# A two-layer convolution block: transforming 32 normalized channels in place of 85 projected ones

## The chip, the core and the metric

The kernel runs on one core of a Trainium2 chip. TensorE (PE) multiplies, VectorE (DVE), ScalarE (ACT) and GpSimd (POOL) do the elementwise work, SyncE (SP) issues most transfers. The metric is device time in microseconds; three runs of the kernel before gave 830.47 (828.88 to 832.42).

## What is computed

Two layers of the same block, each with a residual, on x of shape 4 x 32 x 128 x 128, with HID = 85 and 8 x 8 patches. `_gn` with 32 groups on 32 channels normalizes each channel of each image over its pixels.

```python
def _forward(x, W_in, W_dw, fft_weight, W_out):
    xm = jnp.einsum('bchw,oc->bohw', x, W_in)
    x_spatial, x_freq, x_gate = jnp.split(xm, 3, axis=1)
    out_spatial = depthwise 3x3 convolution of x_spatial with W_dw
    xf = jnp.fft.rfft2(patches of x_freq)
    xf = xf * fft_weight
    xi = jnp.fft.irfft2(xf, s=(P, P))
    out_freq = xi back in image order
    x_fused = jax.nn.gelu(x_gate, approximate=False) * (out_spatial + out_freq)
    return jnp.einsum('bchw,oc->bohw', x_fused, W_out)
...
x = x + layer0(_gn(x)); x = x + layer1(_gn(x))
```

The projection acts on channels and the patch transform on pixels, so the two can be done in either order.

## The kernel before

The image is cut into four bands of 32 columns (Q = 4), and the 128 partitions are 4 bands x 32 channels. A strip is 8 columns wide in each band and 128 rows high; a tile is 16 x 8 = 128 pixels (two patches) of each band. There are 8 tiles in a strip, 32 strips (ALL) and 256 tiles in both layers. All operands of the f16 matmuls are split into a high and a low part, and products of high with high, high with low and low with high are summed.

For each strip DVE normalizes (`normalize`, L812), ACT and DVE split it in three horizontal shifts (L544 and L836, `parts`), and 28 transfers of SP (L273 in pairs, L279 in thirds) put the parts of one band into `stack`, with channels and shifts stacked on 128 partitions. A stack serves as stationary operand, so each tap matmul has the 85 columns of its weights as moving operand. Strip s+1 is loaded from the first step of strip s on, when strip s-1 has left its buffer.

One loop over steps i runs on every engine, each with its own order, with semaphores between them. On PE a step is: taps of band 0 for tile i (`conv(i, 0)`, 7 matmuls, L395); the turned product `ps_ft` of tile i-2 (L442); in each fourth step (i % 4 = 2) the output product `ps_o` of four tiles (L453); half of the gate's projection (L401, `ps_g`); band 1; the projection of the frequency part of tile i+3 (L401, `ps_u`); the rest of the gate; band 2; the patch transform of tile i+2 (L482 to L485, `ps_z`, three matmuls of 340 columns over `uh` and `ul`); band 3; and the inverse transform of tile i into the same bank as the taps (L490 to L493). In short, tile by tile:

- ACT copies `ps_u` scaled to f16 (`uh`, L585) and DVE takes the rest (`ul`, L925).
- DVE multiplies `ps_z` by the weights of the spectrum (`y`, L931), ACT and POOL split that into `yh` (L594) and `yl` (L654) for the inverse.
- ACT applies Gelu (L589), DVE multiplies taps plus inverse by it (`f`, L895), ACT copies the turned product (L579), DVE adds four tiles' output to x (L905) and, in layer 0, takes statistics of them (L774).
- POOL sends and gathers statistics (L616, L622) and edges (L634, L643) in some 15 steps up to step 141.

The last instruction of each step of PE releases the next: `f` of tile i-1 must be done before step i+1 uses the bank, `yl` of tile i+2 before the end of step i+2. At the start the first strip comes in two pieces (`load_piece`) over three queues, and PE runs 32 matmuls of no use (L384) before the loop.

Of the kernel before, what the change touches and what calls it, by code (L numbers as in the profile page):

```python
# [14 lines left out]
LAYERS = 2  # L15
# [25 lines left out]
LEAD = 3  # L41
DRAIN = 4
WARM = 32

OUT = 4
KH = P * (P // 2 + 1)
# [22 lines left out]
FIRST_LOADS = [(PAIRS_HI[0::2], PAIRS_LO[0::2], THIRDS[0::3]), (PAIRS_HI[1::2], PAIRS_LO[1::2], THIRDS[1::3]),  # L69
               ([], [], THIRDS[2::3])]  # L70
# [7 lines left out]
SUMMING = {1: range(8), 2: (17, 21, 24, 25, 29, 32, 33, 37), 3: (49, 53, 56, 57, 61, 64, 65, 69)}  # L78


def build(nc, x_in, edges_in, w_raw, w_fft, w_out, basis, inverse, squares, fold, sums, y_out):
    ctx = ExitStack()
    with ctx:
# [18 lines left out]
        inv = sb("inv", [128, 2, 128], F16)  # L102
        squares_sb = sb("squares_sb", [128, 2, 128])
# [3 lines left out]
        apart = sb("apart", [128, Q, 2 * STRIPS * 6])  # L107
        fold_sb = sb("fold_sb", [KH, 128])

        raw = [sb(f"raw{i}", [128, 12 * HID]) for i in range(LAYERS)]  # L110
        win = [r[:, 0:3 * HID] for r in raw]
        wdw = [r[:, 3 * HID:] for r in raw]
        fft = [sb(f"fft{i}", [KH, HID]) for i in range(LAYERS)]
# [20 lines left out]
        gathered = sb("gathered", [128, Q, 2 * STRIPS * 6])  # L134
        inside = sb("inside", [128, 2])
# [8 lines left out]
        uh = sb("uh", [128, 2, GC], F16)  # L144
        ul = sb("ul", [128, 2, GC], F16)
# [5 lines left out]
        ft = sb("ft", [HID, 2 * OUT, Q, 128])  # L151
# [4 lines left out]
        ps_u = [bank("ps_u0"), bank("ps_u1")]  # L156
        ps_g, ps_z, ps_ft, ps_o = (bank(n) for n in ("ps_g", "ps_z", "ps_ft", "ps_o"))
# [3 lines left out]
        folded = [ps_u[0][:, 0:HID], ps_o[:, 128:128 + HID]]  # L161
# [50 lines left out]
        s_u = sem("s_u")  # L212
        s_uh = sem("s_uh")
        s_ul = sem("s_ul")
# [35 lines left out]
        def staged(i, parts_of_a_strip):  # L250

            if i < 0:
                at = 2 * (i + LEAD)
                return 1, [p for p in parts_of_a_strip.values() if at <= p < at + 2 or i == -1 and p > at]
            strip, at = i // TPS + 2, i % TPS
            return strip, [parts_of_a_strip[at]] if at in parts_of_a_strip and strip < ALL else []
# [40 lines left out]

        def load_piece(eng, piece, by):

            (hi, lo, thirds), loaded = FIRST_LOADS[by], s_first[piece][by]  # L300
# [731 lines left out]
```

## Time and profile before

| | |
|---|---|
| three runs, median | 830.47 us |
| the profiled execution | 829.37 us |
| its span, first to last instruction | 827.6 us |
| PE busy | 799.3 us (97%) |
| DVE busy | 612.7 us (74%) |
| ACT busy | 571.5 us (69%) |
| POOL busy | 274.4 us (33%) |
| mean granted clock of TensorE | 0.993 |

Busy time is that of the engine's own instructions; time spent in waiting or in issuing transfers from SP and ACT does not count. Matmuls are pipelined, each shown longer than the distance to the next one, so the cost of one is read from the distance between starts. A timeline merges equal neighbours, with their count behind the x.

### The profile page before, as it was taken

How to read it: one execution, taken by the hardware profiler on the slowest of the kernel's cores; microseconds unless marked ns; L12 is line 12 of the kernel's file. 1: busy time of each engine (PE TensorE's matmuls, PEld its weight loads, DVE VectorE, ACT ScalarE, POOL GpSimd, SP SyncE). 2: the span in 40 equal slices, each digit the busy share in tenths (PEclk: the TensorE clock that was granted, in tenths of full speed). 3: DMA queues.
4: the chain of work that ended last, by engine and by line, in shares of the span. 5: the costliest groups of instructions: out<-in, count | busy, mean ns of one | idle time of the engine just before them, and what ended most of it. 6: DMA issues, size and time to landing. Idle time of an engine off the chain costs nothing.

```text
span 827.6 us, 31423 instructions
## 1 busy us (share of the span) xinstructions
PE 799.3 (97%) x12332; PEld 654.8 (79%) x12332; DVE 612.7 (74%) x1153; ACT 571.5 (69%) x1149; POOL 274.4 (33%) x345
## 2 busy tenths in 40 slices
PE   1799999999999999999999999999999999999997
PEld 0588888888888888888888888888888888888885
DVE  7887888888888777687777776667667766767553
ACT  2566676767767777777777777677776777777664
POOL 2724232542336322433234223332232333223221
PEclk9799999999999999999999999999999999999999
DMA  8766557545555445655454665655665655566621
GB/s 295 181 210 145 135 125 211 133 113 128 134 125 140 110 111 118 144 132 130 109 118 114 158 141 142 157 131 134 149 141 146 156 133 134 138 142 156 150 63 51
DMA packets 66522, 115.51 MB, mean 140 GB/s; under 512 B 16242, under 2 KB 18954, under 8 KB 65994
## 3 DMA queue, kind: packets, MB, share of 16 engines
q1 hardware_dynamic: 63606, 110.50, 54.1%
q0 software_dynamic: 2144, 2.59, 1.3%
q8 instruction: 99, 1.62, 0.9%
q10 hardware_dynamic: 628, 0.43, 0.2%
q14 instruction: 45, 0.37, 0.1%
HBM read 10.98 MB, written 8.56 MB: 24 GB/s over the span
## 4 chain that ended last, share of the span: by engine, by line
PE 94%; DVE 3%; issue 1%; DMA 1%; ACT 1%; SPq 0%; POOL 0%; DVEq 0%; ACTq 0%
PE ps_s L395 35%; PE ps_ft L442 15%; PE ps_o L453 8%; PE ps_g L401 6%; PE ps_u L401 5%; PE ps_z L482 5%; PE ps_s L490 5%; PE ps_s L493 4%; PE ps_s L491 4%; PE ps_z L485 4%; PE ps_z L483 4%; DMA x<-in_x 1%; DVE parts L836 1%; DVE st L755 0%; DVE amax L685 0%
## 5 line engine op out<-in xcount | busy, mean ns | idle before, releaser
L395 PE MATMUL ps_s<-cw,stack 128*128 128x85 f16 (+1 forms) x7168 | 457.5, 203 | 0.4 <-DVE f L895 0.4
L395 PEld LDWEIGHTS ps_s<-cw,stack 128*128 128x128 f16 (+1 forms) x7168 | 379.4, 98 | 49.1 <-DVE f L895 0.8
L654 POOL TENSOR_TENSOR yl<-y,yh 128x340 f16<-128x340 f32 x256 | 230.0, 899 | 525.4 <-ACT yh L594 525.4
L594 ACT ACTIVATE yh<-y 128x340 f16<-128x340 f32 x256 | 124.7, 487 | 195.6 <-DVE y L931 124.2
L925 DVE SCALAR_TENSOR_TENSOR ul<-ps_u,uh 128x340 f16<-128x340 f32 x256 | 129.7, 506 | 105.6 <-ACT uh L585 104.7
L836 DVE TENSOR_TENSOR parts<-xn,parts 128x1024 f16<-128x1024 f32 (+2 forms) x99 | 118.1, 1198 | 82.3 <-ACT parts L544 82.0
L579 ACT ACTIVATE ft<-ps_ft 85x512 f32<-85x512 f32 x256 | 149.3, 583 | 20.3 <-PE ps_ft L442 16.7
L442 PE MATMUL ps_ft<-squares_sb,f 128*85 128x128 f32 x1024 | 162.6, 281 | 0.8 <-ACT ft L579 0.8
L895 DVE TENSOR_TENSOR f<-ps_s,g 128x340 f32<-128x340 f32 x256 | 129.4, 505 | 12.5 <-PE ps_s L493 4.0
L589 ACT ACTIVATE g<-ps_g,gsc 128x340 f32<-128x340 f32 x256 | 137.6, 537 | 1.2 <-PE ps_g L401 1.0
L931 DVE TENSOR_TENSOR y<-ps_z,weff 128x340 f32<-128x340 f32 x256 | 128.2, 501 | 1.4 <-PE ps_z L485 1.4
L401 PE MATMUL ps_g<-pw,stack 128*128 128x85 f16 x1024 | 125.2, 205 | 0.0
L585 ACT ACTIVATE uh<-ps_u 128x340 f16<-128x340 f32 x256 | 114.5, 447 | 14.3 <-PE ps_u L401 13.2
L401 PEld LDWEIGHTS ps_g<-pw,stack 128*128 128x128 f16 x1024 | 80.2, 98 | 55.3 <-issue 52.8
L442 PEld LDWEIGHTS ps_ft<-squares_sb,f 128*85 128x85 f32 x1024 | 114.8, 155 | 1.0 <-DVE f L895 1.0
L544 ACT ACTIVATE parts<-xn 128x1024 f16<-128x1024 f32 (+2 forms) x99 | 100.3, 1017 | 15.4 <-DVE xn L820 14.2
L401 PE MATMUL ps_u<-pw,stack 128*128 128x85 f16 x1024 | 81.6, 202 | 1.1 <-DVE weff L732 1.1
L482 PE MATMUL ps_z<-uh,bas 128*128 128x340 f16 x256 | 79.2, 309 | 2.6 <-ACT uh L585 1.7
L490 PE MATMUL ps_s<-yh,inv 128*128 128x340 f16 x256 | 79.0, 309 | 0.0
L485 PE MATMUL ps_z<-ul,bas 128*128 128x340 f16 x256 | 78.7, 308 | 0.1
L493 PE MATMUL ps_s<-yl,inv 128*128 128x340 f16 x256 | 78.5, 307 | 0.0
L483 PE MATMUL ps_z<-uh,bas 128*128 128x340 f16 x256 | 78.5, 307 | 0.0
(96 smaller groups left out, 601.7 us busy)
## 6 DMA issues: line engine op xcount, KB each, us to landing
stack<-parts SPq DMA_DIRECT2D x496, 130.0 KB, 2.5
out_y<-yo SPq DMA_DIRECT2D x16, 512.0 KB, 2.8
stack<-parts SPq DMA_DIRECT2D x124, 65.0 KB, 2.1
stack<-parts SPq DMA_DIRECT2D x124, 64.5 KB, 2.1
stack<-parts SPq DMA_DIRECT2D x124, 64.0 KB, 2.0
x<-in_x SPq DMA_DIRECT2D x3, 2048.0 KB, 10.1
x<-in_x SPq DMA_DIRECT2D x4, 512.0 KB, 5.7
raw<-in_w_raw SPq DMA_DIRECT2D x2, 510.0 KB
```

Source lines behind the costliest of these rows:

```text
L395: mm(ps_s[i % 2][:, HID * q:HID * (q + 1)], pixels(kind, i, q, dy, rows), w[0:rows, m, :], start=(q == 0 and m == 0), stop=False)
L401: t = mm(bank[:, HID * q:HID * (q + 1)], pixels(A, i, q, 0), pw[layer(i)][:, which, :], start=(q == 0), stop=(q == Q - 1))
L442: t = nc.tensor.transpose(ps_ft[0:HID, q * 128:(q + 1) * 128], f[:, k, HID * q:HID * (q + 1)], id32)
L482: mm(ps_z[:, 0:GC], bas[:, 0, :], uh[:, k, :], start=True, stop=False)
L579: nc.scalar.activation(ft[:, (i - 2) % (2 * OUT), :, :].rearrange("p q n -> p (q n)"), ps_ft[0:HID, 0:Q * 128], ACT.Copy).then_inc(s_ft, 1)
L589: nc.scalar.activation(g[:, i % 2, :], ps_g[:, 0:GC], ACT.Gelu, scale=gsc[layer(i)][:, 0:1]).then_inc(s_gelu, 1)
L594: nc.scalar.activation(yh[:, i % 2, :], y32[:, i % 2, :], ACT.Copy).then_inc(s_yh, 1)
L654: nc.gpsimd.tensor_tensor(yl[:, k, :], y32[:, k, :], yh[:, k, :], ALU.subtract).then_inc(s_yl, 1)
L836: v.tensor_tensor(part[:, LO, rows], xn[:, rows, 1 + dx:1 + dx + TW], part[:, HI, rows], ALU.subtract).then_inc(s_xl, 1)
L895: v.tensor_tensor(f[:, k, :], ps_s[k][:, 0:GC], g[:, k, :], ALU.mult).then_inc(s_f, 1)
L925: v.scalar_tensor_tensor(ul[:, k, :], ps_u[k][:, 0:GC], US, uh[:, k, :], ALU.mult, ALU.subtract).then_inc(s_ul, 1)
L931: v.tensor_tensor(y32[:, k, :].rearrange("p (q o) -> p q o", q=Q), ps_z[:, 0:GC].rearrange("p (q o) -> p q o", q=Q), weff[layer(i + 2)][:, ...
```

## The change

The transform is applied to the 32 normalized channels (4 bands x 32 = 128 partitions) rather than to the 85 projected ones of each band. For each pair of tiles PE multiplies the split pixels (as stationary operand) by an identity into `ps_xt` (`turn`, four matmuls of 128 columns), DVE copies that to `xt` in f16 (`turned_over`; ACT does so for the first four pairs), and PE transforms it into `ps_x` (`transform`, six matmuls of 128 columns). For each four tiles ACT and DVE split `ps_x` into `xf`, and twelve transfers (`load_spectrum`) stack high, high and low part of one band on 96 partitions of `xs`. The projection then takes four matmuls of 85 columns into `ps_z` (96 rows deep). `ps_u`, `uh`, `ul` and the three matmuls over 340 columns are gone.

In the loop, turns stand in odd steps 2p-11, transforms in the even steps behind them, the split of group h in step 4h-7, its transfers, three in each step, in steps 4h-6 to 4h-3 on POOL ahead of `yl`, and PE first reads the group in step 4h-2. The start is reordered: the first four pairs stand ahead of the loop, which begins one step later (LEAD 2), and the second piece comes over two queues instead of three. Some buffers share memory, and some small steps of layer 1's weights and of the image statistics move by a few steps. The diff, cut to its core:

```diff
-LEAD = 3
+LEAD = 2
 DRAIN = 4
-WARM = 32
+
+WARM = (6, 4, 8, 4, 6)
 
 OUT = 4
+
+PAIR, GROUP = 2, 4
+PAIRS, GROUPS_OF_TILES = TILES // PAIR, TILES // GROUP
+
+SPECTRA = (0, 0, 1)
...
-FIRST_LOADS = [(PAIRS_HI[0::2], PAIRS_LO[0::2], THIRDS[0::3]), (PAIRS_HI[1::2], PAIRS_LO[1::2], THIRDS[1::3]),
-               ([], [], THIRDS[2::3])]
+FIRST_LOADS = [[(PAIRS_HI[0::2], PAIRS_LO[0::2], THIRDS[0::3]), (PAIRS_HI[1::2], PAIRS_LO[1::2], THIRDS[1::3]),
+                ([], [], THIRDS[2::3])],
+               [(PAIRS_HI[i::2], PAIRS_LO[i::2], THIRDS[i::2]) for i in range(2)]]
...
-SUMMING = {1: range(8), 2: (17, 21, 24, 25, 29, 32, 33, 37), 3: (49, 53, 56, 57, 61, 64, 65, 69)}
+SUMMING = {1: range(8), 2: (17, 21, 25, 26, 29, 33, 34, 37), 3: (49, 53, 57, 61, 65, 66, 69, 70)}
...
+        id16 = sb("id16", [128, 128], F16)
...
-        uh = sb("uh", [128, 2, GC], F16)
-        ul = sb("ul", [128, 2, GC], F16)
+
+        xt = sb("xt", [128, PAIR, 2, 128], F16)
+        xf = sb("xf", [128, 2, 2, GROUP * 128], F16)
+        xs = sb("xs", [3 * C, 2, Q, GROUP * 128], F16)
...
-        ps_u = [bank("ps_u0"), bank("ps_u1")]
-        ps_g, ps_z, ps_ft, ps_o = (bank(n) for n in ("ps_g", "ps_z", "ps_ft", "ps_o"))
+        ps_xt, ps_x, ps_g, ps_z, ps_ft, ps_o = (bank(n) for n in ("ps_xt", "ps_x", "ps_g", "ps_z", "ps_ft", "ps_o"))
...
+            if piece == 0:
+                for q in range(Q):
+                    load_spectrum(eng, 0, q, s_xs_first[0][by], (by,))
...
+        def turns_at(p):
+            return PAIR * p - 11 if p >= 8 else p - 4
+
+        def leaves_at(h):
+            return turns_at(2 * h + 1) + 2
+
+        def loads_at(h, q):
+            return 4 * h - 6 + q if h > 2 else (3, 3, 4, 4)[q]
+
+        turning = {turns_at(p): p for p in range(4, PAIRS)}
+        transforming = {turns_at(p) + 1: p for p in range(4, PAIRS)}
+        leaving = {leaves_at(h): h for h in range(2, GROUPS_OF_TILES)}
+
+        def load_spectrum(eng, h, q, loaded, rows=range(3)):
+
+            need(eng, s_z, GROUP * (h - 1))
+            for k in rows:
+                eng.wait_ge((s_xfh, s_xfl)[SPECTRA[k]], h + 1)
+                eng.dma_start(xs[C * k:C * k + C, h % 2, q, :],
+                              xf[C * q:C * q + C, h % 2, SPECTRA[k], :]).then_inc(loaded, 16)
...
+            for q in (0, 1):
+                load_spectrum(sp, 1, q, s_xs_first[1][0])
...
+            pe.wait_ge(s_id16, 1)
+
+            def warm(n):
+
+                for _ in range(n):
+                    mm(ps_ft[:, 0:256], bas[:, 0, :], inv[:, :, :].rearrange("p a n -> p (a n)"), start=True, stop=True)
+
+            def turn(p):
+
+                strip = PAIR * p // TPS
+                pe.wait_ge(s_xl, (1 if p < 2 else 1 + len(ORDER)) if strip == 0 else splits(strip, 0))
+                need(pe, s_xt, p)
+                for j in range(PAIR):
+                    at = TW + PIX * ((PAIR * p + j) % TPS)
+                    for part in (HI, LO):
+                        col = 128 * (2 * j + part)
+                        m = mm(ps_xt[:, col:col + 128], parts[strip % 2][:, part, 1, at:at + PIX], id16[:, :],
+                               start=True, stop=True)
+                m.then_inc(s_xt_made, 1)
+
+            def transform(p):
+
+                pe.wait_ge(s_xt, p + 1)
+                if p % 2 == 0:
+                    need(pe, s_xfh, p // 2)
+                    need(pe, s_xfl, p // 2)
+                for j in range(PAIR):
+                    out = ps_x[:, 128 * ((PAIR * p + j) % GROUP):128 * ((PAIR * p + j) % GROUP) + 128]
+                    mm(out, xt[:, j, HI, :], bas[:, 0, :], start=True, stop=False)
+                    mm(out, xt[:, j, HI, :], bas[:, 1, :], start=False, stop=False)
+                    m = mm(out, xt[:, j, LO, :], bas[:, 0, :], start=False, stop=True)
+                m.then_inc(s_dft, 1)
+
+            for p in range(4):
+                turn(p)
+                warm(WARM[p])
+                transform(p)
+            warm(WARM[4])
...
+            def spectra_loaded(h):
+                if h == 0:
+                    for by in range(3):
+                        pe.wait_ge(s_xs_first[0][by], 16 * Q)
+                elif h == 1:
+                    for by in range(2):
+                        pe.wait_ge(s_xs_first[1][by], 16 * 2 * 3)
+                else:
+                    pe.wait_ge(s_xs[h % 2], 16 * 3 * Q * (h // 2))
...
+                    stacks_loaded(i, 0)
...
-                if live(i, 3):
-                    if begins(i + 3):
-                        stacks_loaded(i + 3, 0)
-                    if (i + 3) % LT == 0:
-                        pe.wait_ge(s_projection, PROJECTIONS * (layer(i + 3) + 1))
-                        pe.wait_ge(s_weff, layer(i + 3) + 1)
-                    need(pe, s_uh, i + 2)
-                    need(pe, s_ul, i + 2)
-                    project(ps_u[(i + 3) % 2], 0, i + 3, range(Q)).then_inc(s_u, 1)
...
+                if i in turning:
+                    turn(turning[i])
...
-                    k = i % 2
-                    need(pe, s_uh, i + 3)
+                    if (i + 2) % LT == 0:
+                        pe.wait_ge(s_projection, PROJECTIONS * (layer(i + 2) + 1))
+                        pe.wait_ge(s_weff, layer(i + 2) + 1)
+                    if (i + 2) % GROUP == 0:
+                        spectra_loaded((i + 2) // GROUP)
                     need(pe, s_y, i + 2)
-                    mm(ps_z[:, 0:GC], bas[:, 0, :], uh[:, k, :], start=True, stop=False)
-                    mm(ps_z[:, 0:GC], bas[:, 1, :], uh[:, k, :], start=False, stop=False)
-                    need(pe, s_ul, i + 3)
-                    mm(ps_z[:, 0:GC], bas[:, 0, :], ul[:, k, :], start=False, stop=True).then_inc(s_z, 1)
+                    col = 128 * ((i + 2) % GROUP)
+                    for q in range(Q):
+                        z = mm(ps_z[:, HID * q:HID * (q + 1)], xs[:, (i + 2) // GROUP % 2, q, col:col + 128],
+                               pw[layer(i + 2)][0:3 * C, 0, :], start=(q == 0), stop=(q == Q - 1))
+                    z.then_inc(s_z, 1)
+                if i in transforming:
+                    transform(transforming[i])
...
+            def turned_over(p):
+
+                act.wait_ge(s_xt_made, p + 1)
+                need(act, s_dft, p)
+                nc.scalar.activation(xt[:, :, :, :].rearrange("p a b n -> p (a b n)"), ps_xt[:, :],
+                                     ACT.Copy).then_inc(s_xt, 1)
+
+            def hi_of_spectrum(h):
+                act.wait_ge(s_dft, 2 * h + 2)
+
+                need(act, s_z, GROUP * (h - 2) + 1)
+                nc.scalar.activation(xf[:, h % 2, 0, :], ps_x[:, :], ACT.Copy, scale=US).then_inc(s_xfh, 1)
+
+            act.wait_ge(s_xn, 2)
+            hi(0, ORDER[0], slice(*PIECES[0]))
+            hi(0, ORDER[1], slice(*PIECES[0]))
+            turned_over(0)
             hi_of_projection(0)
+            hi(0, ORDER[2], slice(*PIECES[0]))
+            turned_over(1)
             hi_of_taps(0)
-            hi_piece(1)
+            hi_of_spectrum(0)
+            for n in range(PROJECTIONS):
+                placing(0, n)
+            act.wait_ge(s_xn, 4)
+            hi(0, ORDER[0], slice(*PIECES[1]))
             load_piece(act, 0, 2)
-            for n in (*range(PROJECTIONS), *range(PLACED - 3, PLACED)):
+            turned_over(2)
+            for n in (6, 10, 11, 12, 13):
                 placing(0, n)
-            load_piece(act, 1, 2)
+            turned_over(3)
+            hi(0, ORDER[1], slice(*PIECES[1]))
+            hi_of_spectrum(1)
+            hi(0, ORDER[2], slice(*PIECES[1]))
...
+                if i in leaving:
+                    hi_of_spectrum(leaving[i])
                 if live(i, -2):
...
-                if live(i, 3):
-                    k = (i + 3) % 2
-                    need(act, s_u, i + 4)
-                    need(act, s_z, i + 2)
-                    nc.scalar.activation(uh[:, k, :], ps_u[k][:, 0:GC], ACT.Copy, scale=US).then_inc(s_uh, 1)
...
+                if i < 0:
+                    for dx in (ORDER[0:1], ORDER[1:])[i + LEAD]:
+                        hi_part(1, dx)
...
             for i in steps():
+                if i in (-1, 0):
+                    load_spectrum(pool, 1, i + 3, s_xs_first[1][1])
+                for h in range((i + 3) // GROUP, (i + 6) // GROUP + 1):
+                    for q in range(Q):
+                        if 2 <= h < GROUPS_OF_TILES and loads_at(h, q) == i:
+                            load_spectrum(pool, h, q, s_xs[h % 2])
                 if live(i, 2):
                     k = i % 2
...
+                for part, groups in ((vh, slice(0, 3 * C)), (vl, slice(C, 2 * C))):
+                    last = v.tensor_copy(cw[0][groups, 0:6, :].rearrange("p (k t) o -> p k t o", k=2),
+                                         part[groups, :, :].rearrange("p (t d) o -> p d t o", d=3)[:, 1:3, :, :])
+                    if part is vh:
+                        link(last)
+                last.then_inc(s_taps, 6)
...
+            def turned_over(p):
+
+                dve.wait_ge(s_xt_made, p + 1)
+                dve.wait_ge(s_dft, p)
+                v.tensor_copy(xt[:, :, :, :].rearrange("p a b n -> p (a b n)"), ps_xt[:, :]).then_inc(s_xt, 1)
+
+            def lo_of_spectrum(h):
+                dve.wait_ge(s_xfh, h + 1)
+                v.scalar_tensor_tensor(xf[:, h % 2, 1, :], ps_x[:, :], US, xf[:, h % 2, 0, :],
+                                       ALU.mult, ALU.subtract).then_inc(s_xfl, 1)
...
+            dve.wait_ge(s_id, 16)
+            v.tensor_copy(id16[:, :], id32).then_inc(s_id16, 1)
...
+            lo_piece(0, ORDER[0])
             scale(0)
+            lo_piece(0, ORDER[1])
             merge(0)
-            lo_piece(0)
+            lo_of_projection(0)
+            lo_piece(0, ORDER[2])
+            lo_of_spectrum(0)
             norm_piece(1)
-            lo_of_projection(0)
+            lo_piece(1, ORDER[0])
+            spectrum(0)
             lo_of_taps(0)
-            lo_piece(1)
             first_taps()
-            spectrum(0)
...
+                if i == 0:
+                    lo_part(1, ORDER[2])
+                if i >= 0:
                     split_beside()
-                if live(i, 3):
-                    k = (i + 3) % 2
-                    need(dve, s_uh, i + 4)
-                    need(dve, s_z, i + 2)
-                    v.scalar_tensor_tensor(ul[:, k, :], ps_u[k][:, 0:GC], US, uh[:, k, :],
-                                           ALU.mult, ALU.subtract).then_inc(s_ul, 1)
+                if i in leaving:
+                    lo_of_spectrum(leaving[i])
+                if i in turning:
+                    turned_over(turning[i])
                 if live(i, 2):
                     k = i % 2
                     need(dve, s_z, i + 3)
@@ -933,12 +1066,17 @@
                                     weff[layer(i + 2)][:, None, :].broadcast_to([128, Q, HID]),
                                     ALU.mult).then_inc(s_y, 1)
...
                 if i == -2:
-                    split_beside()
-                if i == -LEAD:
+                    lo_of_spectrum(1)
+                    lo_piece(1, *ORDER[1:])
+                    norm(1)
+                if i == -1:
+                    lo_part(1, ORDER[0])
+                    lo_part(1, ORDER[1])
+                if i == 1:
                     maxima(1)
-                if i == -1:
+                if i == 3:
                     turned_maxima(1)
-                if i == 2:
+                if i == 5:
                     scales(1)
                     spectrum(1)
```

## Rows read from the trace of the kernel before

**Rows 1.** The page's first part: engine, busy us (share of the span), instructions.
```profile
PE 799.3 (97%) x12332; PEld 654.8 (79%) x12332; DVE 612.7 (74%) x1153; ACT 571.5 (69%) x1149; POOL 274.4 (33%) x345
```
**Rows 2.** Waits: engine, line, released by: us in total, times, longest.
```profile
POOL yl L654 <- ACT yh L594: 525.4, 255, 3.1
...
PE ps_s L395 <- DVE f L895: 0.4, 1, 0.4
```
**Rows 3.** PE's timeline: start us, us, engine, line, operation, tiles, shape, count.
```profile
403.93 0.45 PE L395 MATMUL ps_s<-cw,stack 128*128 128x85 f16 x7
...
405.05 0.32 PE L401 MATMUL ps_u<-pw,stack 128*128 128x85 f16 x4
405.20 0.24 PE L401 MATMUL ps_g<-pw,stack 128*128 128x85 f16 x2
...
405.57 0.31 PE L482 MATMUL ps_z<-uh,bas 128*128 128x340 f16 x1
...
406.00 0.45 PE L395 MATMUL ps_s<-cw,stack 128*128 128x85 f16 x7
...
406.72 0.45 PE L395 MATMUL ps_s<-cw,stack 128*128 128x85 f16 x7
...
409.51 0.45 PE L395 MATMUL ps_s<-cw,stack 128*128 128x85 f16 x7
...
412.25 0.31 PE L482 MATMUL ps_z<-uh,bas 128*128 128x340 f16 x1
...
413.40 0.45 PE L395 MATMUL ps_s<-cw,stack 128*128 128x85 f16 x7
...
418.98 0.45 PE L395 MATMUL ps_s<-cw,stack 128*128 128x85 f16 x7
```
**Rows 4.** DVE's costliest group, shapes apart: busy us, mean ns, idle before.
```profile
L925 DVE SCALAR_TENSOR_TENSOR ul<-ps_u,uh 128x340 f16<-128x340 f32 x256 | 129.7, 506 | 105.6 <-ACT uh L585 104.7
```
**Rows 5.** DVE's timeline in an odd step of layer 0 with output and statistics.
```profile
413.60 0.51 DVE L895 TENSOR_TENSOR f<-ps_s,g 128x340 f32<-128x340 f32 x1
...
415.83 0.50 DVE L931 TENSOR_TENSOR y<-ps_z,weff 128x340 f32<-128x340 f32 x1
```
**Rows 6.** POOL's timeline: four issues in a row, and yl in three kinds of steps.
```profile
153.90 2.19 POOL L622 DMA_DIRECT2D gathered<-sums  x4
...
404.81 1.39 POOL L654 TENSOR_TENSOR yl<-y,yh 128x340 f16<-128x340 f32 x1 [1.85 <-ACT yh L594]
...
414.29 0.83 POOL L654 TENSOR_TENSOR yl<-y,yh 128x340 f16<-128x340 f32 x1 [2.83 <-ACT yh L594]
...
420.72 0.83 POOL L654 TENSOR_TENSOR yl<-y,yh 128x340 f16<-128x340 f32 x1 [2.80 <-ACT yh L594]
```
**Rows 7.** Line 643, POOL's eight transfers of edges between partitions: issue to landing.
```profile
DMA to landing us min/median/max: 1.7/2.1/3.9
```
**Rows 8.** Line 622, POOL's 28 gathers from memory: issue to landing.
```profile
DMA to landing us min/median/max: 1.9/2.3/4.0
```
**Rows 9.** SP's timeline of issues: strip 1, strip 2's pairs, and strip 16.
```profile
33.26 11.34 SPq L273 DMA_DIRECT2D stack<-parts  x16
44.64 7.87 SPq L279 DMA_DIRECT2D stack<-parts  x12
...
60.42 13.58 SPq L273 DMA_DIRECT2D stack<-parts  x16
...
404.12 11.61 SPq L273 DMA_DIRECT2D stack<-parts  x16
415.77 8.55 SPq L279 DMA_DIRECT2D stack<-parts  x12
```
**Rows 10.** ACT's first transfer at the start.
```profile
21.10 0.60 ACTq L279 DMA_DIRECT2D stack<-parts  x1
```

More of the change, by code:

```diff
@@ L155, in build @@
         ps_s = [bank("ps_s0"), bank("ps_s1")]
[L156 to L157 removed]
+        ps_xt, ps_x, ps_g, ps_z, ps_ft, ps_o = (bank(n) for n in ("ps_xt", "ps_x", "ps_g", "ps_z", "ps_ft", "ps_o"))
         turned = [ps_g[0:3, 0:128], ps_o[0:3, 0:128]]
[L161 removed]
+        folded = [ps_z[:, 8:8 + HID], ps_o[:, 128:128 + HID]]
         everywhere = [ps_z[:, 0:3], ps_o[:, 256:259]]
@@ L211, in build @@
                    for i in range(len(PIECES))]
-        s_u = sem("s_u")
-        s_uh = sem("s_uh")
-        s_ul = sem("s_ul")
+        s_id16 = sem("s_id16")
+        s_xt_made = sem("s_xt_made")
+        s_xt = sem("s_xt")
+        s_dft = sem("s_dft")
+        s_xfh = sem("s_xfh")
+        s_xfl = sem("s_xfl")
+        s_xs_first = [[sem(f"s_xs_first_{by}_{h}") for by in ("sp", "pool", "act")] for h in range(2)]
+        s_xs = [sem(f"s_xs{i}") for i in range(2)]
         s_z = sem("s_z")
@@ L296, in load_strip, with count @@
                 load_third(eng, strip, load, s_stk[strip % 2][1])
+        def count(loads, kind):
+            return 16 * (len(loads[0] + loads[1]), len(loads[2]))[kind]
         def load_piece(eng, piece, by):
-            (hi, lo, thirds), loaded = FIRST_LOADS[by], s_first[piece][by]
+            (hi, lo, thirds), loaded = FIRST_LOADS[piece][by], s_first[piece][by]
             first, last = PIECES[piece]
@@ L380, in _ @@
             pe.wait_ge(s_wo, 16 * LAYERS)
-            pe.wait_ge(s_xl, len(ORDER))
-            for k in range(WARM):
-                mm(ps_ft[:, 0:256], bas[:, 0, :], inv[:, :, :].rearrange("p a n -> p (a n)"), start=True, stop=True)
+            pe.wait_ge(s_id16, 1)
[29 more added lines that the diff above has]
+            warm(WARM[4])
             def pixels(kind, i, q, dy, rows=128):
@@ L552, in hi_part @@
                     need(act, s_s, (strip - 2) * TPS + 1)
+                    if strip == 2:
+                        for by, loads in enumerate(FIRST_LOADS[1]):
+                            for kind in range(2):
+                                act.wait_ge(s_first[1][by][kind], count(loads, kind))
                 hi(strip, dx, slice(0, H))
-            def hi_piece(piece):
-                act.wait_ge(s_xn, 2 * piece + 2)
-                for dx in ORDER:
-                    hi(0, dx, slice(*PIECES[piece]))
             act.wait_ge(s_table, 1)
@@ L737, in first_taps @@
                 dve.wait_ge(s_vl, 1)
-                for kind in (A, BB):
-                    for k in range(4):
-                        _, dx, part = GROUPS[k][kind]
-                        v.tensor_copy(cw[0][C * k:C * k + C, 3 * kind:3 * kind + 3, :],
-                                      (vh, vl)[part][C * k:C * k + C, dx + 1::3, :]).then_inc(s_taps, 1)
+                for part, groups in ((vh, slice(0, 3 * C)), (vl, slice(C, 2 * C))):
[4 more added lines that the diff above has]
+                last.then_inc(s_taps, 6)
             def image_stats(b, n):
@@ L951, in _ @@
                             piece(e)
-                for piece, at in ((scale, 53), (merge, 57), (lo_of_projection, 61), (lo_of_taps, 65)):
+                for piece, at in ((scale, 50), (merge, 54), (lo_of_projection, 58), (lo_of_taps, 62)):
                     if i == at:
```

49 lines of the change are left out of this document (20 added, 29 removed).

## The prediction

> **What bounds the kernel now.** I read the page's first part first: PE is busy for 97% of the span, DVE for 74%, POOL for 33% [rows 1]. Busy PE is modelled, so the second view is the list of waits: POOL sat 525 us before its 256 subtractions, while PE's 7168 tap matmuls waited 0.4 us in all [rows 2]. Third comes PE's own timeline [rows 3]. A short step (one tile) runs 403.93 to 406.72, 2.79 us; every fourth step, with the output matmuls of four tiles, runs 409.51 to 413.40, 3.89 us. Nothing in it waits. So the loop is bound by PE's instruction stream: four tiles take 3 x 2.79 + 3.89 = 12.26 us. What the change takes from that stream is gained, unless something new comes last.
>
> **PE: removed and added.** Per tile the four ps_u matmuls go (405.05 to 405.20, 0.15 us) and the three 340-column ps_z matmuls (405.57 to 406.00, 0.43 us) [rows 3]. Four 85-column matmuls replace the latter, at the price of ps_u: 0.15. New are, per pair of tiles, four matmuls that turn pixels (odd steps) and six that transform (even steps), all 128 columns wide. No row has that width in f16. The bounds are its neighbours: 0.15 / 4 = 37.5 ns for 85 columns, 0.43 / 3 = 143 ns for 340. On the line between them 128 columns cost 56 ns; I take that, being much nearer to 85. Ten of them are 0.56 us per pair, 0.28 per tile. A tile thus loses 0.58 and gets back 0.43: 0.15 us. From step 8 to the end: 245 x 0.15 (ps_u) + 246 x 0.28 (ps_z less its successor) = 105.6, less 118 pairs x 0.56 = 66.1, leaves 39.5 us gained. Odd steps become 2.79 - 0.43 + 0.22 = 2.58 us, even ones 2.70, the long one 3.80; four tiles 11.66.
>
> The trace's pairs of weight load and 85-column matmul follow each other every 37.5 ns. [...]
>
> **DVE and ACT.** DVE loses ul, 256 x 0.506 = 130 us [rows 4]. It gets 124 copies of 512 elements from PSUM and 62 subtractions of 512. The nearest row is ul's 0.506 for 340 elements, with PSUM in it too. In proportion 512 would take 0.76, with a fixed part somewhat less; I take 0.65 for both, bounds 0.51 and 0.76: 186 x 0.65 = 121 us. DVE is as busy as before, in a loop 5% shorter, about 77%. Its worst step is odd with output and statistics: before, f started at 413.60 and y at 415.83, with output, statistics and ul between [rows 5]. With the copy in ul's place, 0.2 longer, y starts 2.42 after f, hence at 2.6 into a step of 2.58, and ends 0.5 late. Free time in the next even step absorbs this; f is wanted a full step after it may begin, so PE does not feel it. ACT loses uh, 340 elements in each step, and gets 512 in each fourth: it has more room. Both are hidden; without that cover a late f costs its lateness, in whole.
>
> **POOL and its new loads, where the gain is at risk.** After the start, every transformed spectrum (four tiles) travels by 12 DMAs that POOL issues, three in each step ahead of its subtraction yl. Four issues in a row took 2.19 us, 0.55 each, and yl 0.83 [rows 6]. POOL then does 3 x 0.55 + 0.83 + 0.1 = 2.58 us per step, where a short step lasts 2.58 or 2.70. It fits, but lateness is only recovered in the long step. Queued behind the loads is yl, which has about 3 us of slack. The loads have less. The last three of a group are issued in step 4h-3, after the yl that POOL runs at the head of that step. That yl ended 1.72 us into its step in the plain case (414.29 against 413.40), 2.27 beside DVE's normalization (404.81 against 403.93), and 2.57 where it followed a DVE split (420.72 against 418.98) [rows 3, 6]. For the two kinds of groups I get 2.0 (the hold-up beside the normalization passed on through the next three issues) and 2.25 (2.57 less most of ul's 0.42). The third issue starts 1.1 us later: 3.1 and 3.35. PE wants the data in step 4h-2, a long one, before ps_z: 412.25 - 409.51 - 0.15 = 2.59 into it, so 2.58 + 2.59 = 5.17 after the start of step 4h-3. That leaves 2.07 and 1.82 us from issue to landing.
>
> POOL's small SBUF-to-SBUF DMAs landed after 1.7 to 3.9 us, median 2.1 [rows 7]; those from memory after 1.9 to 4.0, median 2.3 [rows 8]. With 2.1 the two kinds stall 0.03 and 0.28 us, 0.16 on average, times 61 groups: 10 us. In layer 0 the late y of the odd statistics step puts the second kind back by about 0.28 more: 15 x 0.28 = 4 us. Seven groups are followed by four gather issues (2.2 us) of which the long step recovers some 1.3: 6 us. Sends (0.57) and edge copies (0.41) stand directly ahead of last loads 15 times, together some 7 us, of which about 4 meets no room. In all 24 us. Bounds: 4 us with landings of 1.75, about 55 with 2.5; each 0.1 us of landing is 6 us.
>
> Beside DVE, yl took 1.39 instead of 0.83 beside DVE's normalization [rows 6]. [...]
>
> **SP's queue.** A strip's 28 stack loads take 404.12 to 424.32, a landing of some 2 us behind that [rows 9], so 22.3 us in all; a strip of 24.5 becomes 24.5 - 8 x 0.15 = 23.3 us. It still fits, by about 1 us, and only in the thinnest strips not.
>
> **The start.** Before, strip 1's loads begin on SP at 33.26 and strip 2's at 60.42, the moment step 8 begins [rows 9]. In the order of the change four turns and transforms stand ahead of the loop, and turn 2 waits for an ACT copy queued behind eight DMA issues of ACT (about 25 to 30 us, at 0.6 each [rows 10]). Then ACT splits the second piece at about 33 instead of 21; SP can only then issue 14 loads, 6 spectrum loads and strip 1's 28: 33.3 + 20 x 0.64 + 28 x 0.69 = 65.5, landed at 67.0. PE itself would get to step 8 at about 64. Step 8 starts at about 67.0 instead of 60.2: 6.8 us lost, bounds 2 (if ACT's issues run beside its copies) and 9.
>
> **Sum.** The profiled execution's own time is 829.4, 1.1 us under the median of 830.5. 829.4 - 39.5 + 6.8 + 24 = 820.7; I say 821.
>
> **Rivals.** (a) The loads land in time: 829.4 - 39.5 + 6.8 + 4 to 8 = 803. For it: the fastest landing of [rows 7]; against: a margin of only 1.8 to 2.1 us. (b) Slower: POOL falls behind. The place is the last three spectrum loads, the price 0.1 us of lateness for 6 us, and it decides from landings of 2.3 us or issues of 0.62: at 2.5 us the groups stall 0.56, 34 us, with the 14 to 20 of the side jobs 848. For it: the median of [rows 8] and landings up to 4.0; against: these come from memory. (c) The 128-column pairs cost much more than on the line, because a weight load that is not hidden by its matmul is added: at 80 ns, a quarter of the way from 56 to the upper neighbour of 143, PE gives back 118 x 10 x 0.024 = 28 us, of which a third only replaces stalls: about 838. Against: at 85 columns the load is hidden. [...] (d) It does not do what it says, since SP's stack loads come last: 24 more DMAs per strip share the engines with them, and if each of the 28 took 0.08 longer a strip would stay at 24.5 us and the time be 829 and the start's loss less a little, 833. For it: that is 10% of 0.72 [rows 9]; against: 1 us of room.
>
> **How the numbers follow.** Forecast 0.40, (a) 0.24, (b) 0.20, (c) 0.06, (d) 0.10. A measurement of this kernel tells about 0.5% (4 us) from no change. The forecast's own range is 811 to 832, three quarters of it faster by over 4 us. Faster: 0.30 + 0.24 + 0.01 = 0.55; within 0.5%: 0.08 + 0.07 + 0.02 = 0.17; slower 0.28. The range runs from 801 (a) to 845, within (b).
>
> **What would show it.** Right: ps_z's 85-column matmuls are now PE's main wait, ended by a DMA of xs, some tenths of a microsecond per four tiles; POOL about 85% busy; short steps 2.58 and 2.70; step 8 near 67. Wrong: no waits before ps_z (a), waits of 0.5 us and more there (b), longer steps without waits (c), waits before the first tap matmul of a strip on the stack (d), or a start that loses nothing.

## The result, and the profile after

| kernel | median us (lowest to highest) | ratio to before, 95% interval |
|---|---|---|
| before | 829.67 (828.74 to 832.42) | 1 |
| changed | 891.33 (888.09 to 893.86) | 1.0735 [1.0690, 1.0781] |

The change costs 62 us where 9 were forecast as a gain, and the time lies 46 us above the upper end of the range. Here and below, medians and ranges are over all executions, while a ratio leaves out those more than 1.5% above their kernel's fastest (one in each of the first, fifth and eighth experiments). The profiled execution took 890.5, its span is 888.6 (827.6 before), and its mean granted TensorE clock is 0.959 (0.993 before).

The profile page of the changed kernel: first the span with the engines' busy time, their busy tenths and the granted clock in 40 slices, then two of the costliest groups (busy us, mean ns of one, idle before them and its releaser), then two rows of DMA issues (count, KB each, median us from issue to landing).

```profile
span 888.6 us, 32629 instructions
...
PE 790.9 (89%) x12840; PEld 672.8 (76%) x12840; DVE 623.9 (70%) x1080; ACT 515.7 (58%) x963; POOL 637.7 (72%) x1101
...
PEclk9698999989999899998999989999999999999999
...
L357 POOL DMA_DIRECT2D xs<-xf x754 | 377.0, 504 | 13.4 <-DVE xf L975 5.3
...
L567 PE MATMUL ps_z<-pw,xs 96*128 96x85 f16 x1024 | 82.3, 204 | 62.2 <-DMA xs<-xf 61.9
...
stack<-parts SPq DMA_DIRECT2D x496, 130.0 KB, 3.4
xs<-xf POOLq DMA_DIRECT2D x754, 32.0 KB, 2.3
```

PE is busy for fewer microseconds (790.9 where [rows 1] has 799.3), for 89% of its span and no longer for 97%. One group has nearly all of its new idle time: the projection of the transformed spectrum waits 61.9 us for DMAs of xs. In the kernel before, the tap matmuls had waited for 0.4 us in all [rows 2].

The waits of the changed kernel (engine, line, released by: us in total, times, longest):

```profile
POOL yl L770 <- ACT yh L701: 194.7, 186, 4.2
ACT yh L701 <- PE ps_s L579: 165.7, 111, 8.7
...
PE ps_z L567 <- DMA xs<-xf: 61.9, 39, 6.5
```

POOL still waits for 195 us before its subtractions and is 72% busy (85% was forecast), so it is not the bound over the whole; what costs time is 39 single moments. Two groups of four tiles that follow each other, on PE's timeline (start us, us, engine, line, operation, tiles, shape, count, and the idle time before it in brackets). The first group's step 4h-3 begins at 447.66, the second's at 459.41:

```profile
447.66 0.45 PE L474 MATMUL ps_s<-cw,stack 128*128 128x85 f16 x7
...
450.24 0.45 PE L474 MATMUL ps_s<-cw,stack 128*128 128x85 f16 x7
...
452.91 0.33 PE L567 MATMUL ps_z<-pw,xs 96*128 96x85 f16 x4
...
456.71 0.45 PE L474 MATMUL ps_s<-cw,stack 128*128 128x85 f16 x7
...
458.35 0.22 PE L454 MATMUL ps_x<-bas,xt 128*128 128x128 f16 x1
458.41 0.22 PE L455 MATMUL ps_x<-bas,xt 128*128 128x128 f16 x1
458.47 0.22 PE L456 MATMUL ps_x<-bas,xt 128*128 128x128 f16 x1
458.52 0.22 PE L454 MATMUL ps_x<-bas,xt 128*128 128x128 f16 x1
...
459.41 0.45 PE L474 MATMUL ps_s<-cw,stack 128*128 128x85 f16 x7
...
461.99 0.45 PE L474 MATMUL ps_s<-cw,stack 128*128 128x85 f16 x7
...
466.20 0.33 PE L567 MATMUL ps_z<-pw,xs 96*128 96x85 f16 x4 [1.46 <-DMA xs<-xf]
```

The odd step takes 450.24 - 447.66 = 2.58 us and the even one 459.41 - 456.71 = 2.70, as forecast, and matmuls 128 columns wide follow each other every 56 ns. The first group wants its spectrum at 452.91 - 447.66 = 5.25 after the start of step 4h-3 and hardly waits. The second gets it at 466.20 - 459.41 = 6.79.

What differs is the landing. The last three loads of either group, on their line (count, ns of the issue, first and last start; below it issue to landing), the first group's first:

```profile
L357 POOL DMA_DIRECT2D xs<-xf x3: 496/498/512, 450.2 to 451.2; - x3
...
DMA to landing us min/median/max: 1.7/1.8/1.9
```

```profile
L357 POOL DMA_DIRECT2D xs<-xf x3: 496/503/512, 461.7 to 462.7; - x3
...
DMA to landing us min/median/max: 2.9/3.0/3.5
```

The last issue starts 451.2 - 447.7 = 3.5 and 462.7 - 459.4 = 3.3 after the start of the step: POOL is no later in the second group. The slowest of its three transfers needs 3.5 us where the slowest of the first's needs 1.9. SP's timeline and the windows (us, busy us of each engine with counts, granted clock, the DMA engines' busy share, GB/s) say what else is under way:

```profile
445.69 8.04 SPq L293 DMA_DIRECT2D stack<-parts  x12
456.91 12.83 SPq L287 DMA_DIRECT2D stack<-parts  x16
```

```profile
core 0: us, PE busy (x) PEld busy (x) DVE busy (x) ACT busy (x) POOL busy (x), PEclk, DMA share, GB/s
447.66:452.83 5.17, 5.17 (x86) 4.02 (x83) 3.59 (x7) 3.44 (x7) 3.74 (x7) 1.00 0.56 141
459.41:462.90 3.49, 3.49 (x64) 3.18 (x65) 2.64 (x5) 2.49 (x7) 3.47 (x8) 1.00 0.89 213
```

The second group's loads run beside SP's pair loads (line 287, 16 of 130 KB, the engines 89% busy), the first group's beside its smaller thirds (line 293, 56%). A strip has eight steps and a group four, so this alternates: with even h the last loads are issued in step 5 of a strip, with odd h in step 1. I took the start of every group's first ps_z matmul against the start of its step, less the 2.59 us of a step that doesn't wait: 56 us of the 70 found so, over 62 groups, are in odd h, 14 in even h. The last landing of a group takes 3.4 us in the median with odd h and 1.8 with even h, and POOL starts that load 3.1 and 3.2 us into step 4h-3.

The longest stalls cost more than their own length. PE's timeline and the windows behind a wait of 3.58 us:

```profile
516.34 0.45 PE L474 MATMUL ps_s<-cw,stack 128*128 128x85 f16 x7
520.36 0.47 PE L567 MATMUL ps_z<-pw,xs 96*128 96x85 f16 x4 [3.58 <-DMA xs<-xf]
...
521.26 0.71 PE L474 MATMUL ps_s<-cw,stack 128*128 128x85 f16 x7
```

```profile
520.38:523.00 2.62, 2.62 (x26) 2.22 (x27) 0.99 (x4) 0.08 (x1) 0.00 (x0) 0.50 0.89 210
...
526.50:529.20 2.70, 2.70 (x51) 2.54 (x49) 1.66 (x5) 2.35 (x4) 1.75 (x3) 1.00 0.35 85
```

Behind the wait the granted clock is 0.50, and 26 matmuls run in the time in which 51 run later. The same sixteen matmuls (six of a transform, seven taps, three of the inverse) take 2.00 us there, from 520.62 to 522.62, and 1.05 later, from 528.17 to 529.22. Behind the shorter wait at 466.20 the clock stayed at 1.00. Of the fifteen waits of 1.6 us and more from step 8 on, twelve (the shortest 1.64) have a granted clock of 0.50 at their end or just behind it, three (2.28, 2.13 and 2.16) do not.

The balance: the span rose by 61.0. The start lost 8.9 (step 8 begins at 69.1, before at 60.2), the loop's own work gained 39.5 by the forecast's sum, which the step lengths bear out, and PE waited 61.9 for xs. 61.0 - 8.9 + 39.5 - 61.9 leaves 30 us. Where they lie can be read from the steps. From step 8 on the steps are 92 us longer than they are without waits (2.58, 2.70 and 3.80 us, and less by the turns and transforms in the last ten): 62 of these are waits, 24 lie in steps with a granted clock below 1, and the other 6 are mostly some 0.17 us per wait, since a matmul is shown longer than it takes (an 85-column one 0.20 us, with the next start 0.04 later) and the idle time behind it shorter. The mean clock fits that: 888.6 x 0.041 = 36.4 us were not granted, before 827.6 x 0.007 = 5.8, hence 31 more, of which 3 are in the start and some passed while PE stood still.

### The profile page after: what moved, and what is told of

Same layout as the page of the kernel before. It is cut to its first block, busy times and chain, and to the rows that moved or that the text cites. A ratio compares the mean times of both kernels' runs of the same rounds, so it can differ in the third digit from the quotient of the medians.

```text
span 888.6 us, 32629 instructions
## 1 busy us (share of the span) xinstructions
PE 790.9 (89%) x12840; PEld 672.8 (76%) x12840; DVE 623.9 (70%) x1080; ACT 515.7 (58%) x963; POOL 637.7 (72%) x1101
## 4 chain that ended last, share of the span: by engine, by line
PE 38%; POOL 16%; DMA 15%; DVE 11%; issue 10%; ACT 8%; ACTq 1%; DVEq 0%; POOLq 0%
DMA xs<-xf 14%; PE ps_s L474 14%; POOL xs L357 8%; POOL yl L770 7%; PE ps_ft L529 6%; PE ps_z L567 3%; DVE y L1064 3%; PE ps_s L579 2%; PE ps_s L576 2%; PE ps_s L577 2%; ACT yh L701 2%; PE ps_g L480 2%; ACT turned_results L691 2%; PE ps_o L540 2%; PE ps_xt L442 2%
## 5 line engine op out<-in xcount | busy, mean ns | idle before, releaser
L357 POOL DMA_DIRECT2D xs<-xf x754 | 377.0, 504 | 13.4 <-DVE xf L975 5.3
L953 DVE TENSOR_TENSOR parts<-xn,parts 128x1024 f16<-128x1024 f32 (+2 forms) x99 | 122.3, 1237 | 85.5 <-ACT parts L630 85.3
L529 PE MATMUL ps_ft<-squares_sb,f 128*85 128x128 f32 x1024 | 168.4, 288 | 0.9 <-ACT turned_results L691 0.9
L691 ACT ACTIVATE turned_results<-ps_ft 85x512 f32<-85x512 f32 x256 | 149.5, 584 | 25.8 <-PE ps_ft L529 24.5
L567 PE MATMUL ps_z<-pw,xs 96*128 96x85 f16 x1024 | 82.3, 204 | 62.2 <-DMA xs<-xf 61.9
L529 PEld LDWEIGHTS ps_ft<-squares_sb,f 128*85 128x85 f32 x1024 | 119.5, 160 | 1.3 <-DVE f L1028 1.0
L567 PEld LDWEIGHTS ps_z<-pw,xs 96*128 96x128 f16 x1024 | 54.3, 99 | 68.7 <-DMA xs<-xf 67.4
L971 DVE CAST xt<-ps_xt 128x512 f16<-128x512 f32 x124 | 84.7, 683 | 11.9 <-PE ps_xt L442 10.2
L576 PE MATMUL ps_s<-yh,inv 128*128 128x340 f16 x256 | 80.8, 316 | 0.0
L577 PE MATMUL ps_s<-yh,inv 128*128 128x340 f16 x256 | 80.4, 314 | 0.0
L975 DVE SCALAR_TENSOR_TENSOR xf<-ps_x,xf 128x512 f16<-128x512 f32 x64 | 44.3, 691 | 37.5 <-ACT xf L661 37.5
```

What stands on the lines that cost most here:

```text
L357: eng.dma_start(xs[C * k:C * k + C, h % 2, q, :], xf[C * q:C * q + C, h % 2, SPECTRA[k], :]).then_inc(loaded, 16)
L529: t = nc.tensor.transpose(ps_ft[0:HID, q * 128:(q + 1) * 128], f[:, k, HID * q:HID * (q + 1)], id32)
L567: z = mm(ps_z[:, HID * q:HID * (q + 1)], xs[:, (i + 2) // GROUP % 2, q, col:col + 128], pw[layer(i + 2)][0:3 * C, 0, :], start=(q == 0), s ...
L691: nc.scalar.activation(ft[:, (i - 2) % (2 * OUT), :, :].rearrange("p q n -> p (q n)"), ps_ft[0:HID, 0:Q * 128], ACT.Copy).then_inc(s_ft, 1)
L953: v.tensor_tensor(part[:, LO, rows], xn[:, rows, 1 + dx:1 + dx + TW], part[:, HI, rows], ALU.subtract).then_inc(s_xl, 1)
```

## The experiments

All of them start from the changed kernel, except the seventh.

**Which neighbour makes the landing long.** Theory: SP's pair loads. Rival: the place of the group in the loop (what POOL and DVE do in steps 1 and 2 of a strip). The first experiment swaps SP's two kinds of loads within each strip and leaves POOL, DVE and PE alone.

```
+            eng.wait_ge(s_xl, splits(strip, ORDER.index(-1)))
+            for load in THIRDS:
+                load_third(eng, strip, load, s_stk[strip % 2][1])
...
             for load in PAIRS_LO:
                 load_pair(eng, strip, load, s_stk[strip % 2][0])
-            eng.wait_ge(s_xl, splits(strip, ORDER.index(-1)))
-            for load in THIRDS:
-                load_third(eng, strip, load, s_stk[strip % 2][1])
```

> SP issues the 12 third loads of each strip (65 KB) ahead of the 16 pair loads (130 KB); nothing else changes. Theory A (the last spectrum loads land late because SP's burst of pair loads has the DMA engines): the pair loads now start some 8 us later in a strip, so the 3.4 us landings of the group that is read in the strip's step 2 become about 2 us and its waits, 56 us of 69, shrink to under 20, while those of the group read in step 6 grow from 13 to 30 or more. Rival B (POOL is late by its own work, or DVE's normalization holds its descriptors up, both of which keep their place in the strip): the waits stay in step 2, 50 us or more. In total A 860 to 890 us, B 891.

Measured: 903.03 us (892.99 to 911.08), ratio 1.0845 [1.0778, 1.0912]. The stalls changed sides: by the same count as above, 56 us are now in even h and 17 in odd h. The total of 860 to 890 was missed, since the even groups now lose as much as the odd ones did; the profiled execution, the fastest of four, has a span of 891.1, and what makes the others slower is open. Two groups of this kernel, odd h (issued beside thirds) and even h (beside pairs):

```profile
L357 POOL DMA_DIRECT2D xs<-xf x3: 496/496/512, 454.2 to 455.2; - x3
...
DMA to landing us min/median/max: 1.7/1.7/2.0
```

```profile
L357 POOL DMA_DIRECT2D xs<-xf x3: 496/498/512, 466.3 to 467.3; - x3
...
DMA to landing us min/median/max: 2.6/2.9/4.0
```

The place in the loop is what it was and the landings have swapped; over all groups the median of the last landing went from 1.8 to 3.4 us with even h and from 3.4 to 1.9 with odd h. That shows the cause of the regular stalls: the neighbours in the DMA engines, and not POOL's own work in that place.

**Earlier loads.** If 1.5 to 2 us more from issue to use are enough, the stalls should go.

```
-            return 4 * h - 6 + q if h > 2 else (3, 3, 4, 4)[q]
+            return 4 * h - 6 + (0, 0, 1, 2)[q] if h > 2 else (3, 3, 4, 4)[q]
```

> POOL issues the spectrum loads of a group in steps 4h-6 (six), 4h-5 and 4h-4 (three each) instead of three in each of four steps, so that the last have one step, 2.7 us, more to land. Both theories put the loss into the wait for xs; with 2.6 to 2.7 us of margin more, waits above that in the changed kernel's trace are few (the one of 6.5 us in strip 2, gather groups): about 10 us left of 69, and 5 of the 21 us that the halved clock behind the waits cost: 810 to 820 us. If POOL's throughput were the bound, the waits would only move to yl before the inverse transform and the time stay above 860 us.

Measured: 839.05 us (836.73 to 840.53), ratio 1.0112 [1.0092, 1.0132]: 52 us gained by one line. But 810 to 820 was missed by 19 us, and the kernel is still 1% slower than the one before. Its waits (as above):

```profile
POOL gathered L732 <- DMA sums<-st: 8.0, 3, 5.4
PE ps_s L579 <- POOL yl L770: 6.7, 5, 3.8
...
PE ps_z L567 <- DMA xs<-xf: 16.1, 10, 4.0
```

The stall in every second group is gone and ten single ones are left, with a new kind: the inverse transform waits for yl. The transfers did not become faster (the last landing with odd h is still 3.3 us in the median); they only have more time.

**No spectrum loads at all.** What do the loads cost in all, and what is a 128-column matmul worth? From the fifth group on nothing is loaded, and the projection reads what the first groups left, so the output is not the reference's from there on.

```
-                    pe.wait_ge(s_xs[h % 2], 16 * 3 * Q * (h // 2))
+                    pe.wait_ge(s_xs[h % 2], 16 * 3 * Q)
...
-                        if 2 <= h < GROUPS_OF_TILES and loads_at(h, q) == i:
+                        if 2 <= h < 4 and loads_at(h, q) == i:
```

> Leaves out the spectrum loads from the fifth group on (PE goes on reading what the first groups left there), so what it computes from there on is not the reference's. POOL and the DMA engines are as in the kernel before. It gives PE's stream alone: 829.7 - 39.5 + 8.9 for the start = 799 us if 128-column matmuls cost 56 ns; 827 if they cost 80.

Measured: 812.49 us (811.14 to 812.78), ratio 0.9791 [0.9776, 0.9805]; span 809.2. The loads thus cost 891.3 - 812.5 = 79 us, waits and clock together. 799 was missed by 13 us. 6.0 of them are one wait that was left in, that of a group which still loads (step 10):

```profile
L567 PE MATMUL ps_z<-pw,xs 96*128 96x85 f16 x1024 | 81.0, 202 | 6.8 <-DMA xs<-xf 6.0
```

With it, 827.6 + 8.9 - 39.5 + 6.0 = 803 for the span. Of the other 6, by the lengths of the steps, 2.5 lie in steps at a granted clock below 1 behind that wait, 1.2 in other waits of PE, and the rest in steps that are some tenths longer. A matmul of 80 ns, as in rival (c), would have added 28 us.

**The start.** ACT splits the whole second piece ahead of its own DMA issues, and DVE its part ahead of the loop, both on top of the earlier loads (ACT's two hi(0, ...) of the second piece behind the turns go; DVE's lo_piece and norm of strip 1 move from step -2 to ahead of the loop).

```
-            hi(0, ORDER[0], slice(*PIECES[1]))
+            for dx in ORDER:
+                hi(0, dx, slice(*PIECES[1]))
             load_piece(act, 0, 2)
```

> As the kernel with early loads, and in the start ACT splits all of the second piece before its own DMA issues, and DVE takes the rest of that piece and the normalization of strip 1 ahead of the loop. SP can then issue the second piece's loads from about 29 us instead of 32.5, and strip 1's from about 42 instead of 45.85; step 8 starts near 65 instead of 69.1. 4 us under the kernel with early loads alone, about 810 us. Rival: PE is the one that is late in the start, and step 8 stays at 69.

Measured: 836.35 us (834.52 to 838.23), ratio 1.0082 [1.0059, 1.0105]. Step 8 begins at 67.9, not 65, so 1.3 of the hoped-for 4 us were got in the start (2.7 in the median time), and the 810 of the forecast, which hung on the second experiment's, was missed by 26.

Two kinds of stall in this kernel show where the rest is. At 155.9 PE waits 4.05 us for loads that POOL had issued nine microseconds earlier:

```profile
L357 POOL DMA_DIRECT2D xs<-xf x3: 498/502/508, 146.8 to 147.8; - x3
...
DMA to landing us min/median/max: 6.8/6.8/8.1
```

```profile
141.16 0.58 SPq L369 DMA_DIRECT2D x<-in_x  x1
```

```profile
147.00:155.00 8.00, 4.86 (x77) 3.56 (x76) 4.18 (x7) 4.16 (x8) 5.84 (x11) 0.89 1.03 236
```

SP had issued an image of 2 MB, and over those 8 us the DMA engines' share was 1.03. And at 297.88 the inverse transform waits 4.22 us for yl; POOL's timeline before it:

```profile
289.27 0.60 POOL L731 DMA_DIRECT2D gathered<-sums  x1 [1.14 <-DMA sums<-st]
292.38 1.64 POOL L731 DMA_DIRECT2D gathered<-sums  x3 [2.51 <-issue]
294.01 2.96 POOL L357 DMA_DIRECT2D xs<-xf  x6
296.99 0.84 POOL L769 TENSOR_TENSOR yl<-y,yh 128x340 f16<-128x340 f32 x1
```

The gathers wait for the sums, 2.51 us more pass between the first gather and the other three (the profile shows nothing that POOL waited for), then six loads are issued at once, and yl stands behind all of it.

**Images in quarters.** Images 2 and 3, on top of the fourth experiment's edits; DVE waits for the quarter that it needs (not shown).

```
-                    load_image(2)
-                if strip == 4:
-                    load_image(3)
+                if strip <= 2 * STRIPS:
+                    load_quarter(2 + (strip - 1) // STRIPS, (strip - 1) % STRIPS)
```

> The kernel of e4, with images 2 and 3 loaded in eight pieces of 512 KB, one behind each of the first eight strips' stack loads, in place of two of 2 MB behind strips 1 and 4. Theory (the engines' queues are full while a 2 MB image passes, and the spectrum loads beside it land after 8 us): in e4 the matmuls on the spectrum waited 2.8 us at step 10, 4.2 at step 34, 2.4 at step 42; step 10 and 34 go, with the halved clock behind them some 10 us are gained: 826. Rival (these waits are of POOL's own queue, which at steps 9 and 37 has four gather issues more): nothing changes, 836 within 2.

Measured: 827.06 us (820.88 to 835.38), ratio 0.9962 [0.9939, 0.9986]. The stalls at steps 10 and 34 are gone, as the theory says; one of 2.5 us is new at step 18, where a load issued at 99.3, beside pairs, landed after 5.3. The waits for xs fell from 14.7 to 9.7 us. POOL's queue was the same, so the rival falls.

**Gathers issued by SP.** On top of the fifth experiment's edits.

```
-                    if i == at + READ:
-                        gather(e)
...
+            gathers(eng, strip, 0)
             eng.wait_ge(s_xl, splits(strip, ORDER.index(-1)))
             for load in THIRDS:
                 load_third(eng, strip, load, s_stk[strip % 2][1])
+            gathers(eng, strip, 1)
```

> e5 with the 28 gather DMAs issued by SP (ahead of the last twelve or behind all loads of a strip) in place of POOL. Theory (POOL, whose queue the new loads fill, pays for its side jobs: the gather waits for the landing of the sums, 1 to 2.5 us, and issues for 2.2 us, with the subtraction behind it; in e4 the inverse matmuls then waited 1.3 at step 41, 1.7 at 44, 1.7 at 72, 4.5 at 76, 0.9 at 104 and 0.85 at 136, with the clock behind it some 14 us): 8 to 14 us below e5, about 815. Rival (SP is as full as POOL, and its strip comes later by 2.4 us): the waits reappear before the taps that read the third pass, e5 within 3 us.

Measured: 809.96 us (808.76 to 815.18), ratio 0.9780 [0.9747, 0.9813]: faster than both kernels, and 17 us below the fifth experiment where 8 to 14 were expected. Its waits:

```profile
PE ps_z L586 <- DMA xs<-xf: 3.4, 6, 0.9
PE ps_s L493 <- DMA stack<-parts: 3.4, 3, 1.7
...
PEld ps_s L598 <- POOL yl L781: 1.6, 1, 1.6
```

The rival was right that SP's strips come later, but only three times, for 3.4 us in all (once, for 1.0, in the fifth experiment). Its landings of xs are no shorter (median 2.6 us, 2.3 in the changed kernel); they only have more time.

**Are the side jobs the whole story, or worth something alone?** Two controls: both side edits on the kernel before, and both on the changed kernel with its loads where they were.

> The kernel before with the two edits of e5 and e6 alone (images 2 and 3 in quarters, gathers issued by SP) and nothing of the change. Theory (these edits only take away waits that the change had brought; the tap matmuls and the transform of the kernel before waited for nothing): 828 to 831, the same as before. Rival (they are worth something by themselves, and e6 owes its time partly to them): below 825.

Measured: 830.38 us (827.25 to 831.55), ratio 1.0007 [0.9991, 1.0022]. The edits are worth nothing where nothing waited, so the 2.2% by which the sixth experiment's kernel is faster than the kernel before are not their own: they come with the transform of 32 channels, once its loads are early enough.

> The changed kernel with the two edits of e5 and e6 alone; its last spectrum loads stay in step 4h-3, 2 us ahead of their use. Theory (the 1.4 us by which those loads land late beside SP's pair loads come in every second group and do not hang on the side jobs): e4 lost 29 us less to images and gathers when they were moved, and of that after has about the half, since the side jobs' waits there run into the same stalls: 865 to 878, still slower than before. Rival (the side jobs were the cause all along and the place of the loads did little): 815 to 830.

Measured: 878.59 us (876.01 to 891.02), ratio 1.0587 [1.0563, 1.0612], at the upper edge of the 865 to 878 expected. Without the earlier loads the same edits bring 13 us; with them, from 836.35 to 809.96, they bring 26. So the place of the loads is the first cause (52 us), and images and gathers the second.

## Why the prediction was wrong

- *PE's work*: right. Steps of 2.58 and 2.70 without waits, 56 ns for 128 columns: rival (c) falls (its own terms add up to 840, not 838). Its 80 ns was an estimate that no run shows; the trace has 56 ns with a weight load for each (12840 matmuls and 12840 loads).
- *DVE*: 0.65 forecast for copy and subtraction, measured 0.683 and 0.691. Hidden, as said, in the loop.
- *POOL's issues*: 0.55 forecast, 0.504 measured, also beside the new copies from PSUM: 212 of the issues ran beside such a copy, and none of them took more than 0.51; beside DVE's normalization the longest took 0.84. The last issue starts 3.1 to 3.2 after its step in the median (3.3 and 3.5 in the two groups shown), forecast 3.1 and 3.35; PE wants it at 5.2, forecast 5.17. The margin of 1.8 to 2.1 us was right.
- *Landing*: the step that failed. I took 2.1 us, the median of [rows 7], for all groups. All eight transfers of [rows 7] are issued late in a strip (the first at 81.25, in step 14), where SP issues its small loads or none, and with even h the last landings are mostly 1.7 to 2 us indeed. The last loads of odd h are issued in step 1, beside the pairs, and the median of their last landings is 3.4. The sum itself says what that does: 1.3 us more in half of the groups is 31 x 1.3 = 40 us on top of 24, together 64, and the waits came to 61.9. That the two are so near is in part luck, since the sum goes by medians, and landings in the odd groups run from 1.7 to 8.2.

The kernel before had a warning in it, a weaker one than the effect. [rows 8] mixes both places: its twelve gathers beside pairs landed after 2.7 us in the median, the sixteen late in a strip after 2.2. Its line taken apart gives, for a gather in step 10, beside pairs, and for one in step 70, late in its strip, the following (the kernel before, issues at 68.8 and at 252.1):

```profile
L622 POOL DMA_DIRECT2D gathered<-sums x4: 548/554/569, 68.8 to 70.4; - x4
...
DMA to landing us min/median/max: 2.7/2.9/3.7
```

```profile
L622 POOL DMA_DIRECT2D gathered<-sums x4: 548/552/561, 252.1 to 253.7; - x4
...
DMA to landing us min/median/max: 2.2/2.3/2.4
```

I set the landings up to 4.0 aside with "these come from memory", although [rows 7], which moves data between partitions, reaches 3.9. But these longest ones do not fit the neighbours either: in the kernel before, 4.0 (issued at 155.5), 3.7 (156.1) and 3.9 (179.1) stand late in a strip, with the engines 15 to 17% busy in the 4 us behind. What made them long is open.

- *The clock*: missing from the sum. I priced a stall at its length. Twelve stalls, of 1.64 to 6.5 us, had the clock at 0.50 behind them, and the steps there lost some 24 us more, over a third of what the stalls themselves took.
- *Rival (b)* named the right place, the last three loads, and the right sign, with 0.20. Its price for a landing of 2.5 us was 848; with 3.4 in half of the groups and the clock it is 891. I had capped the range at 845, just under (b)'s own price for 2.5 us, though [rows 7] and [rows 8] reached 4.
- *The start*: 6.8 forecast, 8.9 measured, by another way. SP's strip 1 loads were issued until 66.2 (forecast 65.5), but PE itself was as late: five waits for DVE, of 4.73, 1.22, 1.25, 0.99 and 0.77, sum to 9.0 (from the first tap matmul to step 8; before, two of 0.81 and 0.42). The first stands before a turn that wants the strip which DVE is still splitting:

```profile
40.00 0.61 PE L442 MATMUL ps_xt<-id,parts 128*128 128x128 f16 x4 [4.73 <-DVE parts L953]
```

- *SP's queue* (d): the pairs' landing rose from 2.5 to 3.4, but the taps did not wait for the stack in the changed kernel. Right as forecast.

What stays open: the 24 us of the clock are read from the lengths of the steps in one trace, and no run took the low clock away and left the stalls. Nor does any run show what made the longest landings of the kernel before.

## What to carry to other kernels

Read a transfer's landing time at the place in the loop where the new transfers will run, with the DMA engines' share there beside it; a median over all places hides the one that stalls (2.3 us over all loads here, 3.4 for the last ones of the odd groups). A load that is issued just in time on a path without slack should be moved ahead first: one line was worth 52 us of the 62 lost here, and the change was worth having (2.2%) only when the images and gathers had been moved too. And when an engine's queue is filled with new issues, its old side jobs (a wait for a transfer, four issues in a row) become visible and want another queue (17 us here).

## What the hardware showed that I had not expected

A 32 KB transfer between partitions landed after 1.8 us with the DMA engines 56% busy, after 3.0 at 89%, and after 6.8 to 8.1 beside a 2 MB load, with the share at 1.03. POOL's issue time stayed at 0.50 us in all three. Over all 744 such loads of the loop, sorted by the engines' share in the 2 us from their issue, the median landing is 2.0 us below 0.7, 2.6 from 0.7 to 0.9 and 3.1 above. The 130 KB loads suffered too: 2.5 us before, 3.4 with the small ones beside them, and 2.5 again in the run without them, though POOL's queue moves only 27.4 of the 140.8 MB of the whole kernel. Behind a wait of PE of 3.6 us the granted clock was 0.50 and the spacing of 128-column matmuls went from 56 to 110 ns (they start at 520.62, 520.73, 520.84); behind one of 1.5 us it stayed at 1.00. The length of the wait alone does not decide: 0.50 came with one of 1.64 and not with one of 2.28.
